# Cross attention and expert layer: a later first gather, earlier statistics and weight halves, another group order in the last expert

## The reference

```
x = x + cross_attention(layernorm(x), ctx, ctx)          # 16 heads, 77 keys
ln1 = layer_norm(x);  qkv, scores, attn, ao = ...        # 8 x 8 causal attention over the first axis
h1 = x + ao @ proj
z = layer_norm(h1);   logits = z @ router_weight         # 4096 tokens, 8 experts
top_p, top_i = top_k(softmax(logits), 2)
# tokens are placed in order into 1280 places per expert, the rest is dropped
fc1 = gelu(xt @ moe_w1);  fc2 = fc1 @ moe_w2             # per expert, 512 -> 1024 -> 512
out = h1 + scatter_add(fc2 * padded_probs)
```

## Time and profile before

| what | us |
|---|---|
| median of 3 runs | 1536.03 |
| lowest, highest | 1532.99, 1536.2 |
| the profiled execution, its own time | 1534.42 |
| its span in the trace | 1532.6 |
| PE busy | 1460.8 |
| DVE, POOL, ACT busy | 924.2, 821.8, 724.8 |
| granted TensorE clock, mean | 0.983 |

### The profile page before, as it was taken

One profiled execution on the slowest core, in us unless ns is written; L12 is line 12 of the kernel. 1 busy time (PEld: TensorE's weight loads), 2 busy tenths in 40 slices (PEclk: granted clock), 3 DMA queues, 4 the chain that ended last, 5 costly groups with the idle time before them and its releaser, 6 DMA issues. The chain is left out here.

```text
span 1532.6 us, 30182 instructions
## 1 busy us (share of the span) xinstructions
PE 1460.8 (95%) x11079; PEld 1303.6 (85%) x11079; DVE 924.2 (60%) x1758; ACT 724.8 (47%) x1467; POOL 821.8 (54%) x942
## 2 busy tenths in 40 slices
PE   8999899999999999899859999999999999999997
PEld 7678788888888888788749989989999889998985
DVE  4876687777778876888665355443332654353362
ACT  4555555655555555566515354433332544343341
POOL 2445555566666656686625365552533776255233
PEclk9999999999999999999959999999999999999999
DMA  7212211122222122222223252443423444243222
GB/s 271 81 64 70 90 56 63 66 73 73 83 77 70 60 67 70 84 83 91 97 71 97 59 125 71 98 110 71 101 53 67 112 112 105 50 112 71 48 35 26
DMA packets 64295, 125.76 MB, mean 82 GB/s; under 512 B 13337, under 2 KB 13721, under 8 KB 63628
## 3 DMA queue, kind: packets, MB, share of 16 engines
q1 hardware_dynamic: 45932, 93.81, 18.2%
q0 software_dynamic: 17920, 29.31, 11.3%
q10 hardware_dynamic: 288, 0.52, 0.1%
HBM read 89.06 MB, written 46.27 MB: 88 GB/s over the span
## 5 line engine op out<-in xcount | busy, mean ns | idle before, releaser
L1582 PE MATMUL hidden_ps<-gT,w 128*128 128x256 f32 x2880 | 354.1, 285 | 8.1 <-ACT hT L1484 3.6
L1582 PEld LDWEIGHTS hidden_ps<-gT,w 128*128 128x128 f32 x2880 | 351.1, 192 | 12.0 <-ACT hT L1484 4.2
L1609 PE MATMUL expert_ps<-w,hT 128*128 128x512 f32 x1440 | 335.7, 392 | 0.0
L1609 PEld LDWEIGHTS expert_ps<-w,hT 128*128 128x128 f32 x1440 | 268.3, 188 | 55.8
L1353 POOL TENSOR_TENSOR w<-raw,w 128x1024 fp32r<-128x1024 f32 x62 | 152.8, 2519 | 248.2 <-ACT w L1347 248.2
L1509 DVE TENSOR_TENSOR hT<-gl,hT 128x512 fp32r<-128x512 f32 x160 | 126.0, 795 | 221.4 <-ACT hT L1484 221.4
L1482 ACT ACTIVATE gl<-hidden_ps 128x512 f32<-128x512 f32 x160 | 95.8, 599 | 299.7 <-PE hidden_ps L1582 261.9
L1461 POOL DMA_INDIRECT out_dram<-og,idx x76 | 123.4, 1624 | 65.1 <-DVE og L1537 45.3
L1537 DVE TENSOR_SCALAR og<-expert_ps,kept 128x512 f32<-128x512 f32 x78 | 58.0, 749 | 159.5 <-PE expert_ps L1609 146.8
L1492 ACT ACTIVATE gT<-yk 128x256 fp32r<-128x256 f32 x160 | 66.9, 418 | 129.0 <-DVE yk L1520 127.0
L1448 POOL DMA_INDIRECT xg<-normed_tokens,idx x78 | 85.9, 1102 | 54.7 <-POOL idx L1443 30.2
(11 more groups left out here) (192 smaller groups left out, 3111.5 us busy)
## 6 DMA issues: line engine op xcount, KB each, us to landing
raw<-L_ffn_moe_w_dram SPq DMA_DIRECT2D x64, 512.0 KB, 3.7
normed_tokens<-h SPq DMA_DIRECT2D x128, 65.0 KB
xa<-x_dram SPq DMA_DIRECT2D x32, 256.0 KB, 2.7
xc<-x_dram SPq DMA_DIRECT2D x32, 256.0 KB, 3.0
attended_rows<-x SPq DMA_DIRECT2D x32, 256.0 KB, 2.1
fx<-attended_rows SPq DMA_DIRECT2D x128, 64.0 KB
out_dram<-fx SPq DMA_DIRECT2D x128, 64.0 KB
fx<-qkv_rows_dram SPq DMA_DIRECT2D x1, 1536.0 KB, 7.3
```

Source lines behind the costliest of these rows:

```text
L1582: last = pe.matmul(pH[:, q, f * W:(f + 1) * W], w1[p][l][:, k, cols], xT[g.s % 2][r][:, k, :], start=k == 0 and n == 0, stop=k == KT - 1 a ...
L1609: last = pe.matmul(pY[:, k, :], hT[par][l][:, f, k * P:(k + 1) * P], w2[p][r][:, f, :], start=f == 0 and n == 0, stop=f == FT - 1 and n == 2)
```

## The change

It has six edits.

1. The first group's gather moves from the end of the first part to the start of the second, behind the barrier.
2. `EASED` = 35 takes the place of `LATE` = 38 in `stats_f` and `factors`: in steps 36, 37 and 38 they stand early in the lists.
3. Pieces 3 to 7 of the first expert's weights are loaded one step earlier, and POOL makes the low halves of pieces 0 to 5 in the middle of the step after their high half (behind `shared2`, the second attention's shares, ahead of `weighed`) and no longer at the end of the same step.
4. `LATE_LOW` is empty: the low half of piece 6 moves from DVE's step 49 to the second part, ahead of that of piece 7.
5. In steps 5, 7 and 9 `xT_lo` is made ahead of the maximum and no longer behind it.
6. The last expert takes its groups in the order 4, 3, 2, 1, 0: turns 0, 1 and 2 are then empty, turns 3 and 4 are not.

```
-FIRST_PIECES = {LATE: (0,), LATE + 2: (1,), LATE + 4: (2,), LATE + 6: (3,), LATE + 7: (4,), LATE + 8: (5,),
-                LATE + 9: (6,), LATE + 10: (7,)}
-LATE_LOW = {LATE + 11: 6}
+EASED = NT + LP - 1
+FIRST_PIECES = {LATE: (0,), LATE + 2: (1,), LATE + 4: (2,), LATE + 5: (3,), LATE + 6: (4,), LATE + 7: (5,),
+                LATE + 8: (6,), LATE + 9: (7,)}
+LATE_LOW = {}
...
-                if i > LATE:
+                if i > EASED:
                     factors(i)
...
+                for j in FIRST_PIECES.get(i - 2, ()):
+                    if j < 6:
+                        weights["low"](pool, 0, 0, j)
+                if FF < i <= EASED:
                     factors(i)
...
-                for j in FIRST_PIECES.get(i - 1, ()):
-                    if j < 6:
-                        weights["low"](pool, 0, 0, j)
             pool.wait_ge(s["xg_cleared"], 1)
-            for n in range(4):
-                pool.wait_ge(z2_out[n], 64 * (NT // 4))
-            pool.wait_ge(s["rows_done"], 1)
-            for k in range(GB):
...
-                if i > LATE:
+                if i > EASED:
                     stats_f(i)
...
                         chained(dve.tensor_tensor(scores, scores, m, ALU.add))
+                        if i % 2 == 1 and i >= LP:
+                            low_normed(i + 1)
...
 TURN = (3, 2, 1, 0, 4)
+LAST_TURN = (4, 3, 2, 1, 0)
...
-    at = At(g.c, g.off - turn + TURN[turn], PER)
+    last = PER * g.c + g.off >= NG - GPE
+    at = At(g.c, g.off - turn + (LAST_TURN if last else TURN)[turn], PER)
...
-                    for k in range(0 if opening else GB):
+                    for k in range(GB):
                         pool.indirect_dma_start(out=xg[:, g.s % 2, k, :], out_offset=None, in_=z2d[:, :],
...
                 if isinstance(c, int) and c == 0 and i == 4:
-                    low(dve, 0, 0, CH - 1)
+                    dve.wait_ge(s["w_lo"], CH - 2)
+                    for j in (CH - 2, CH - 1):
+                        low(dve, 0, 0, j)
```

More of the change, by code:

```diff
@@ L148, in build @@
                           "og": own("og", [P, GB, D])}
-                groups["gathered"] = [[sem(f"e_gathered{i}_{k}") for k in range(GB)] for i in range(2)]
             with scratch:
@@ L329, in build_main @@
                  "lg_mm lg_evac cleared dve_link pool_link "
-                 "consts_done counted gap gap_exp weighed prefixed blks hots tabled xg_cleared rows_done").split()
+                 "consts_done counted gap gap_exp weighed prefixed blks hots tabled xg_cleared").split()
         s = {n: sem(n) for n in names}
@@ L571, in _ @@
                         .then_inc(s["shared2"], 1)
-                if FF < i <= LATE:
+                for j in FIRST_PIECES.get(i - 2, ()):
+                    if j < 6:
+                        weights["low"](pool, 0, 0, j)
+                if FF < i <= EASED:
                     factors(i)
@@ L888, in write_rows @@
                 chained(dve.tensor_tensor(token, token, negative, ALU.add))
-                dve.tensor_copy(row_table[:, :], token).then_inc(s["rows_done"], 1)
+                chained(dve.tensor_copy(row_table[:, :], token))
             for k in range(KT):
@@ L1014, in _ @@
                     for half in range(2):
-                        if i <= FF and half == (0 if t < S else 1):
+                        if i <= FF and half == (0 if t < S else 1) and not (t < S and i % 2 == 1 and i >= LP):
                             sooner(i + 1)
@@ L1061, in _ @@
                     dve.tensor_tensor(gap[:, f % 2:f % 2 + 1], tops[:, f, 1:2], tops[:, f, 0:1], ALU.subtract).then_inc(s["gap"], 1)
-                if i <= LATE:
+                if i <= EASED:
                     stats_f(i)
@@ L1379, in build_experts @@
         scattered = [sem(f"e_scattered{k}") for k in range(GB)]
-        gathered = groups["gathered"]
+        gathered = [[sem(f"e_gathered{i}_{k}") for k in range(GB)] for i in range(2)]
         block = st.enter_context(nc.Block())
```

## The result

| | before | after |
|---|---|---|
| median of 7 runs | 1536.0 us (1533.0 to 1539.2) | 1541.6 us (1539.3 to 1542.3) |
| profiled execution, its span | 1534.4, 1532.6 us | 1541.7, 1539.9 us |
| DVE, POOL busy | 924.2, 821.8 us | 933.7, 820.9 us |

After over before is 1.0037, with a 95% interval of 1.0028 to 1.0046: 5.7 us slower. The forecast was 3.4 us slower (1539.4) and its range held the result. The sum is nearly right, its terms are not: one term has the wrong sign, and two others gave more than foreseen. Among the executions of the kernel before that were taken beside the last two experiments, one took 2049.3 us at a granted clock of 0.65; it is left out.

What follows compares the result with a forecast made beforehand. TensorE, busy almost throughout, was taken as the bound, so edits count by its gaps: 0.2 - 2.7 - 0.9 - 0.9 - 0.7 + 8.4 = +3.4 us, giving 1539.4 us, range 1533.5 to 1543.5.

Steps and rivals of the forecast that it cites:

- The last expert: Second part's end: full group 38 waits behind a third empty group's skip, released by group 35's scaling; plus 8.4 us.
- clock: Last expert's matmuls after the long gap: TensorE loses 2.0 us at half clock, bounds 0 and 2.9.
- tail: After TensorE's end: one full scatter ends the span, 9.8 us after TensorE instead of 11.4; 1.6 less.
- The faster rival: Last expert: third empty group costs only one gelu round, TensorE starts at 1479.5; all by -3.2, 1532.8 us; chance 0.13.
- xT_lo: Steps 5, 7, 9: TensorE waits for pr, not xT_lo, so no gain; plus 0.2 us in all.
- Statistics: Steps 36 to 38: early statistics remove TensorE's waits before z, less DVE's limit and an fx wait; minus 2.7 us.
- Weight halves: Low halves in mid-step: fx waits of steps 41 and 43 go, part returns in 42 and 44; minus 0.9 us.
- Piece 6: Step 49: DVE's 1.24 us ahead of the last but one residual sum goes; minus 0.9 us.
- the first part gives back more: First part's last steps: less idling keeps the clock up, 1 to 3 us more off; change 0, 1536; chance 0.17.
- Gather: Barrier: first gather behind it, barrier opens 1.6 us after the table, second transfer lands 3.1 later; minus 0.7 us.
- its own sign of being wrong: Up to the table: a first part shorter by under 2 or over 8 us would show the forecast wrong.
- the first part gives less: First part: statistics meet fx's load every step, weight halves only move waits; gains 2.5, change +5.9, 1541.9; chance 0.15.

Runs made afterwards that it cites:

- the last two experiments: Kernel before with last expert's order 3, 2, 1, 4, 0: 1546.1 us; order 4, 3, 2, 1, 0 with DVE's scaling of group 35 ahead of turning group 38: yk to end 740.98.

## Why the prediction was right or wrong

**The last expert: right.** Forecast +8.4; the stretch says +8.2, the kernel with that edit alone +8.3. Its parts: start 8.9 us later, measured 8.8 (pause 10.67 against 1.85); clock 2.0, measured 1.3 (13.09 against 11.75); the transposes that now lie in the pause minus 0.9, as measured; tail minus 1.6, measured minus 1.5. That the skip waits for the scaling of the empty group is what the rows say: the start follows it by 1.2 us in the whole change and in the order alone, and followed a scaling by 1.07 before. But the transposes end only 0.2 us ahead of the scaling, and no run has a start that the scaling alone decides. One sign of being right, a single idle time of 9 to 10 us ended by og, didn't come. The faster rival (one round of gelu) needed a start before 1480 and falls.

**xT_lo: right**, nothing that the time shows; the waits in steps 6, 8 and 10 are 0.1 us longer each.

**Statistics: right in kind, a little too large.** The step of the prediction that was off: "without it DVE needs about 11.6". The steps take 12.5 now. I took DVE's durations as they stood and charged a wait for fx of 1.1 us that didn't come; what came was a hold of up to 0.9 us on aT_lo in each step, since POOL's z product moved onto it. Minus 2.7 forecast, minus 2.2 in the stretch.

**Weight halves: wrong in sign.** The term was minus 0.9 with plus 1.0 as its upper bound; the stretch shows +3.4. I reasoned from POOL's list alone and priced DVE's operations as if they ran free of POOL. That a half delays the shares by some 1 us was right (1.77 against 0.78), but I took the delay as harmless where it pushes POOL's z product onto aT_lo. And the half that before ran beside statistics with one input and sums on the matmul banks now runs beside subtractions, comparisons and the z scaling from SBUF. The Trainium skill (SBUF — State Buffer, Who interferes with whom) states it: a VectorE instruction with two SBUF inputs contends with a GpSimd instruction that reads SBUF, and one with at most one such input, outside the two-port modes, doesn't. The rows agree: the subtraction of two tensors is held (1.52), written with one it isn't (0.21), the maximum isn't (0.17). The z scaling of 128x512 has one tensor as input and was held all the same (1.67 instead of 0.55); by this rule it would have to run in a two-port mode, and no row here shows that. I had weighed another sentence of that page, on transfers, and not this one. The trace of before even had it: the subtraction at 0.64 us in step 39, beside POOL's product of the second attention's shares (658.28, 1.05 us), and aT_lo at 0.85 in step 37, against 0.16 and 0.69.

**Piece 6: right**, 0.93 for 0.9. Behind it the clock gave back some 1.5 more (27.71 to 26.15 us), which is the mechanism of my rival "the first part gives back more" in its last steps. Where it applies is open: the halves alone have the same shorter pause of 1.05 us and still fall to the half clock.

**Gather: too small.** Minus 0.7 forecast, minus 1.5 in the stretch. From the table's end at 792.69 the second transfer is issued 3.3 us later where I took 3.8, since the barrier opens 1.0 after the table and not 1.6; and from that issue to yk it takes 4.0 where I took 4.2. The eight transposes run without a pause from 797.95, so the second block had landed by about 798.9, 2.9 us after its issue. My 3.1 was a little long; the Trainium skill's estimate, which I had given as 2.6 us, isn't excluded by that row.

**The first part as a whole: its own sign of being wrong came.** A first part that is shorter by under 2 us up to the table was to show the prediction wrong. It is 0.6 longer, and 1.4 shorter without the 2.0 ahead of step 36. The number measured, +5.7, is that of my rival "the first part gives less" (+5.9), but not by its mechanism: the statistics met no load of fx, and the weight halves didn't only move waits, they cost time.

So the sum of +3.4 was near the measured 5.7 partly by luck: weight halves 4.3 worse and statistics 0.5, gather 0.8 better and the clock 1.5. The profiled execution of before was also one of the quicker ones ahead of step 36, so the difference of spans, 7.3, overstates the change.

## What to carry to other kernels

Before moving an operation of GpSimd, list what VectorE does beside it at the old place and at the new one: here what reads two tensors from SBUF, and the scaling of 128x512 from SBUF to SBUF, was held until GpSimd's operation ended, and the hold hides in a duration, where no list of waits shows it. Look as well at what stands behind the moved operation in GpSimd's list: a step later it may fall on an instruction that ran free. Removing the held instruction only passed the hold on to the next; move the holder. And where groups can be empty, count those ahead of the last full ones: here two left a pause of 1.85 us and the third made it 10.7. An empty one between the full ones cost more (11.5 us against 8.3), with 4.4 of it at the half clock.

## What was not expected of the hardware

- TensorE's clock after the same pause isn't the same in each execution. Behind the wait of 2.3 us near 216 us one execution ran at the half clock and another at the full one. The whole change and the kernel with all but the order have the same code there, and only the first ran at the half clock. The stretch up to step 36 takes from 607.0 to 610.9 us in twelve executions whose code there is the same but for xT_lo. Single spans therefore compare to some 4 us at best. Stretches do better, and not all alike: with the same code steps 36 to 39 and table to yk agree within 0.1 us, but steps 39 to 47, 47 to the table and yk to the end only within 1.0 to 1.4.
- A shorter pause ahead of the same matmuls can go with the full clock: with 1.06 us idle ahead of the last step's matmuls they ran in 0.27 us each, with 1.96 in 0.38 to 0.42; but with 1.05 they were slow too in the kernel with the halves alone. What decides was not tried.
